# Statistics of x1 moved from the front of the scan's tile to its middle, and the last four normalisations shared between VectorE and ScalarE

## The reference, cut to what matters

```python
x = layernorm(x + attn(x))       # attn: h = x + mamba2(rmsnorm(x)); h + relu(rmsnorm(h) @ w_fc)**2 @ w_proj
x = layernorm(x + ffn(x))        # ffn: silu(x@w1)*(x@w2), two 1024x1024 gelu layers, @ w3
layernorm: (x - mean) / sqrt(var + 1e-5), over the 256 columns of a row
```

## Time and profile before

| what | us |
|---|---|
| median of 3 runs (1225.24 to 1225.66) | 1225.28 |
| the profiled execution, its own time | 1226.21 |
| its span, first to last instruction | 1224.5 |
| scan: one tile of the hardware loop | 66.6 |
| scan and its head, up to the FFN phase | about 568 |
| TensorE busy over the span | 1195.6 |
| VectorE busy over the span | 783.8 |
| GpSimd busy over the span | 237.7 |
| granted clock of TensorE, mean | 0.996 |

### The profile page before, as it was taken

One profiled execution on the slowest core, in us unless ns is written; L12 is line 12 of the kernel. 1 busy time (PEld: TensorE's weight loads), 2 busy tenths in 40 slices (PEclk: granted clock), 3 DMA queues, 4 the chain that ended last, 5 costly groups with the idle time before them and its releaser, 6 DMA issues.

```text
span 1224.5 us, 19168 instructions
## 1 busy us (share of the span) xinstructions
PE 1195.6 (98%) x6412; PEld 1003.1 (82%) x6412; DVE 783.8 (64%) x1370; ACT 639.2 (52%) x1199; POOL 237.7 (19%) x210
## 2 busy tenths in 40 slices
PE   8899999999999999999999999999999999999996
PEld 7677888888887888788888888888888888888885
DVE  6798898989999898855535337345363363543633
ACT  6687888878788878666224124142141331422420
POOL 0517253443435261720000000000000000000000
PEclk9999999999999999999999999999999999999998
DMA  8214131333324141334500202002002020020000
GB/s 294 71 65 126 65 81 72 105 99 101 105 78 128 58 124 64 99 128 172 211 1 1 52 1 51 0 0 51 0 6 45 0 51 0 0 51 0 18 1 19
DMA packets 92169, 79.40 MB, mean 65 GB/s; under 512 B 63200, under 2 KB 81760, under 8 KB 90208
## 3 DMA queue, kind: packets, MB, share of 16 engines
q1 hardware_dynamic: 92128, 78.86, 20.8%
HBM read 66.77 MB, written 25.70 MB: 76 GB/s over the span
## 4 chain that ended last, share of the span: by engine, by line
issue 53%; POOL 0%; DVE 0%; POOLq 0%; DVEq 0%
POOL rsv_b L1937 0%; DVE o_sb L2014 0%; POOLq L1935 0%; DVEq L1768 0%; POOL rsv L237 0%; POOLq L450 0%
## 5 line engine op out<-in xcount | busy, mean ns | idle before, releaser
L1921 ACT ACTIVATE full<-bank,scale 128x512 f32<-128x512 f32 x128 | 88.3, 690 | 383.0 <-PE bank L1830 383.0
L1830 PE MATMUL bank<-hB_hi,h_sb 128*128 128x512 f32 x512 | 199.6, 390 | 0.0
L1830 PE MATMUL bank<-hB_lo,h_sb 128*128 128x512 f32 x512 | 199.6, 390 | 0.0
L1830 PE MATMUL bank<-hA_hi,h_sb 128*128 128x512 f32 x512 | 199.3, 389 | 0.0
L1830 PE MATMUL bank<-hA_lo,h_sb 128*128 128x512 f32 x512 | 199.3, 389 | 0.0
L1983 DVE CAST hA_hi<-full 128x512 fp32r<-128x512 f32 x64 | 27.3, 427 | 173.1 <-ACT full L1921 173.1
L1937 POOL TENSOR_TENSOR rsv_b<-mv_b,eps 128x4 f32<-128x4 f32 x8 | 10.7, 1340 | 618.2 <-DVE mv_b L189 618.2
L1830 PEld LDWEIGHTS bank<-hA_hi,h_sb 128*128 128x128 f32 x512 | 96.1, 188 | 20.1
L1830 PEld LDWEIGHTS bank<-hA_lo,h_sb 128*128 128x128 f32 x512 | 96.1, 188 | 20.1
L1830 PEld LDWEIGHTS bank<-hB_hi,h_sb 128*128 128x128 f32 x512 | 96.3, 188 | 19.2
L1830 PEld LDWEIGHTS bank<-hB_lo,h_sb 128*128 128x128 f32 x512 | 96.2, 188 | 19.0
(11 more groups left out here) (231 smaller groups left out, 2967.6 us busy)
## 6 DMA issues: line engine op xcount, KB each, us to landing
chk_xh<-w_ffn SPq DMA_DIRECT2D x16, 704.0 KB, 4.2
ffn_raw<-w_ffn SPq DMA_DIRECT2D x8, 1408.0 KB, 7.0
h_sb<-ffn_raw SPq DMA_DIRECT2D x2, 4096.0 KB, 19.0
xT<-x_t SPq DMA_DIRECT2D x8, 512.0 KB, 3.9
x_res<-x SPq DMA_DIRECT2D x8, 512.0 KB, 3.8
x_rows<-x SPq DMA_DIRECT2D x8, 512.0 KB, 3.5
x_in<-x_rows SPq DMA_DIRECT2D x8, 512.0 KB, 4.7
x_in<-x SPq DMA_DIRECT2D x7, 512.0 KB, 4.7
```

What stands on the lines that cost most here:

```text
L1830: ins = pe.matmul(o, a_, b_, start=first and n == 0, stop=last and n == 1, skip_group_check=True)
L1921: nc.scalar.activation(full[:, n % FULL, :], b[:], ACT.Gelu, scale=scale[:, 1 + n // KH, n % KH:n % KH + 1]).then_inc(s_gd, 1)
```

## The change

Scan: `norm_x1` leaves the front of DVE's iteration. Its four `bn_stats` (`stats_x1`) and its seven small instructions (`norm_x1_tail`) go, one right behind the other, between `add_out 1` and `yT 2`. On POOL `x1_rstd` goes from between `decay 1` and `u 2` to between `m_lo 6` and `ud 3`. This holds for tiles 2 to 7. `norm_x1` stays as it is for tile 6 (after the scan) and tile 7 (in the FFN phase).

Last FFN tile: the mean's sign is turned (the sum is multiplied by -0.5), so that DVE adds it; DVE scales chunks 0, 1 and 2; POOL computes one more small product, mean times reciprocal deviation (`shift_b`), and ACT scales chunk 3 as `Identity(x * rsv + shift)`. SPq's second store waits for DVE's third chunk and for ACT's.

```diff
@@ POOL, iteration
                     decay_state(i, 1)
-                    if norm:
-                        x1_rstd(pool, i - 2)
                     make_u(w, i, 2)
...
                     if mlp:
                         m_lo_part(i - 1, 6)
+                    if norm:
+                        x1_rstd(pool, i - 2)
                     if more:
                         make_ud(w, i, 3)
@@ DVE, iteration
-                    if norm:
-                        norm_x1(dve, i - 2)
                     mask_exponents(w, 0)
...
                     add_out(w, i, 1)
+                    if norm:
+                        x1_step = stats_x1(dve, i - 2)
+                    if norm:
+                        norm_x1_tail(x1_step)
                     yT(w, 2)
@@ new on DVE
+        def stats_x1(dve, t):
+            step = Steps(dve, s_ls, STAT_STEPS * t)
+            dve.wait_ge(s_pjd, CH * t + CH + 1)
+            for c in range(CH):
+                step.mark(nc.vector.bn_stats(bn[:, c, :], x1[:, c, :]))
+            return step
+        def norm_x1_tail(step):
+            step.wait(step.n)
+            layer_norm_tail(step, bn, mv, EPS_LN).then_inc(s_mv, 1)
@@ SP, last tile
-                    sp.wait_ge(s_o, CH * i + 2 * n + 2)
+                    sp.wait_ge(s_o, CH * i + 2 + n)
+                    if n == 1:
+                        sp.wait_ge(s_oact, 1)
@@ ACT, end
+                act.wait_ge(s_rsb, TILES + 1)
+                c = CH - 1
+                nc.scalar.activation(o_sb[:, c, :], o_sb[:, c, :], ACT.Identity, scale=rsv_b[:, c:c + 1],
+                                     bias=shift_b[:, c:c + 1]).then_inc(s_oact, 1)
@@ POOL, end
+                pool.wait_ge(s_rsb, TILES)
+                nc.gpsimd.tensor_tensor(shift_b[:], mv_b[:, 0, :], rsv_b[:], ALU.mult).then_inc(s_rsb, 1)
@@ DVE, finish_last
-                    layer_norm_tail(step, bn_b, mv_b, EPS_LN).then_inc(s_mvb, 1)
+                    layer_norm_tail(step, bn_b, mv_b, EPS_LN, -0.5).then_inc(s_mvb, 1)
                     dve.wait_ge(s_rsb, i + 1)
-                    for c in range(CH):
+                    for c in range(CH - 1):
                         nc.vector.tensor_scalar(o_sb[:, c, :], o_sb[:, c, :], mv_b[:, 0, c:c + 1], rsv_b[:, c:c + 1],
-                                                ALU.subtract, ALU.mult).then_inc(s_o, 1)
+                                                ALU.add, ALU.mult).then_inc(s_o, 1)
```

More of the change, by code:

```diff
@@ L179, in layer_norm_stats, with layer_norm_tail @@
             return layer_norm_tail(step, bn, mv, eps)
-        def layer_norm_tail(step, bn, mv, eps):
+        def layer_norm_tail(step, bn, mv, eps, half=0.5):
             tt, ts = nc.vector.tensor_tensor, nc.vector.tensor_scalar
@@ L185, in layer_norm_tail @@
             step.link(tt(mv[:, 1, :], bn[:, :, 2], bn[:, :, 5], ALU.add))
-            step.mark(ts(mv[:, 0, :], mv[:, 0, :], 0.5, None, ALU.mult))
+            step.mark(ts(mv[:, 0, :], mv[:, 0, :], half, None, ALU.mult))
             step.mark(tt(mv[:, 2, :], mv[:, 2, :], mv[:, 2, :], ALU.mult))
@@ L227, in sum_x1 @@
                     scalar=r2h[:, c:c + 1], in1=xh[:, c, :], op0=ALU.mult, op1=ALU.add).then_inc(s_pjd, 1)
+        def stats_x1(dve, t):
[7 more added lines that the diff above has]
+            layer_norm_tail(step, bn, mv, EPS_LN).then_inc(s_mv, 1)
+            assert step.n == STAT_STEPS
         def norm_x1(dve, t):
@@ L1744, in post_ln_block @@
         bn_b, mv_b = sb("bn_b", [P, CH, 6]), sb("mv_b", [P, 3, CH])
-        rsv_b = sb("rsv_b", [P, CH])
+        rsv_b, shift_b = sb("rsv_b", [P, CH]), sb("shift_b", [P, CH])
         g_bank = lambda i: banks[i % B_ACT_BANKS]
@@ L1765, in post_ln_block @@
         s_o = sem("out_ready")
+        s_oact = sem("last_rows_out_ready")
         s_store = sem("out_stored")
```

## The result

The changed kernel takes 1234.28 us (median of 4, 1232.21 to 1235.66) against 1225.26 (4 runs, 1224.04 to 1225.66): ratio 1.0073, 95% interval 1.0058 to 1.0088. It is slower, as forecast (1232.6, range 1225.0 to 1236.0). The profiled execution took 1233.96, its span is 1232.3 us against 1224.5.

A forecast was written before the change was run, and what follows sets the result against it. TensorE, busy 98% of the span, bounds the kernel, so only its gaps, set by DVE and POOL holding each other up, can move. 5 x (0.62 + 0.88) - 0.2 = +7.3 on 1225.28 gives 1232.6 us, range 1225.0 to 1236.0.

The forecast's parts named there:

- Part 1, gain at `ydiag 0`: Front of the loop tile: 3.12 us leaving DVE only becomes waiting for POOL's `decay 0`; gain 0, at most 0.23.
- Part 1, `u 2` ahead of `scores 1`: Front: without `x1_rstd`, `u 2` runs first; `scores 1` +0.85, `norm_x` -0.23, so PE loses 0.62 us a tile.
- Part 2: Middle of the loop tile: late POOL instructions hold up DVE's add L1479 and a tap; +0.88 us a tile at `fc0`.
- The work itself is hidden: Middle: the 2.26 us added to DVE fit before `y_diag 3`; `yT 2` ends at 338.8, ahead of 339.06.
- Part 3: End of the kernel: three DVE scalings instead of four end 0.32 us sooner; -0.2 us in the sum.
- B: Rival, chance 0.14: only the middle costs; L1479 gets in ahead of `ud 1` and pays for `scores 1`; 1229.5 us.
- E: Rival, chance 0.11: faster, 1219.5 us; at the front L1479 gets ahead of `ud 1` and `scores 1` ahead of `u 2`.
- C: Rival, chance 0.14: only the front costs; in the middle POOL's two instructions fall between DVE's; 1228.2 us.
- F: Rival, chance 0.08: in the middle one more POOL instruction comes ahead of DVE, 1.88 us a tile; 1237.6 us.

The follow-up runs named there:

- the stand-in: The changed kernel plus an unused POOL power on four columns ahead of `u 2`, where `x1_rstd` had stood: 1228.62 us, ratio 1.0020.
- the last experiment: The kernel before the change with two POOL waits: `ud 1` behind the second add of `y_diag 0`, `u 3` behind `xn_lo`; 1223.7 us, ratio 0.9986.
- 8: The changed kernel with the seven small statistics instructions behind gate 3 on DVE and `x1_rstd` behind `decay 3` on POOL: 1231.6 us, ratio 1.0058.
- 9: The changed kernel with the small statistics instructions behind gate 3, `x1_rstd` behind `decay 3`, and an unused POOL power ahead of `u 2`: 1227.91 us, ratio 1.0023.

## Why the prediction was right

**Part 1, gain at `ydiag 0`: 0.** Right. `scores 0` hangs on POOL's `decay 0`.

**Part 1, `u 2` ahead of `scores 1`: +0.85 - 0.23 = +0.62.** Right in mechanism and size: +0.85 and -0.25 by the rows, 0.61 at PE, 0.58 back with the stand-in, 0.62 with the power alone moved. Only the place was off: PE's loss shows in front of `ydiag 1`, while the gap at L678 shrinks to 0.34 and the one at L592 stays 0.88; the prediction had both grow. It left out that PE itself waits for `scores 1`.

**Part 2, +0.88.** Right mechanism, mis-sized. The two collisions came as forecast (0.27 for 0.3, 0.78 for 0.85; the gate 1.02 late for 1.15), but the slack from the gate to `fc0` is 0.40 and not 0.18 + 0.08. Measured: +0.61. The prediction also let PE lose it all at `fc0`; part of it comes earlier, at the transposes of h (gap of 0.56). "The work itself is hidden" held as well, since it filled idle time; the runs add that the same small instructions put behind that idle time aren't hidden (0.37 and 0.42 a tile), and that taking the collision away gives back 0.24 only.

**Part 3, -0.2.** Wrong in sign in the profile (+0.26), and nothing that a time can tell. ACT's instruction was fast enough; the term that the sum missed is the second wait in front of the store, 0.34 us of issue. ACT started 0.04 us after POOL's product had ended, and its timeline shows no table load in the 8.85 us ahead of it. The Trainium skill (ScalarE: Activation LUTs, Table sets: the hidden batching unit) has identity in every set, and the trace agrees.

**The sum.** 5 x (0.62 + 0.88) = 7.5 was forecast for the loop; 5 x 1.23 = 6.15 measured, by the tiles at full clock. That the time came out 1.7 above the forecast in spite of it has other sources: in the profiled execution some 1.3 of the stretch at lower clock (69.37 - 68.08), and 0.67 of tile 7, the way into the FFN and the end. So the mechanism was right, and that the time lies within 2 us of the forecast is in part luck: a loop put 1.35 too high takes off nearly half of some 3 us that no term of the sum had.

Against the scan part alone (6.5 us) the whole change (9.0) has 2.5 us more, and the end alone shows nothing; the intervals of the two ratios overlap, and the executions of the changed kernel were granted mean clocks of 0.992 to 0.997 where the kernel before had 0.994 to 0.998 beside the last experiment. Stretches at lower clock differ from execution to execution and are worth as much. In the windows of 10 us up to 50 us six of the fourteen traces have them, the kernel before (0.83) and the one after (0.79, 0.86) among them; the scan part alone has 0.52 from 40 to 50, and its first `sum_x1` comes at 162.03, where the eight traces without such a stretch have it between 155.6 and 157.4. But which executions of the changed kernel had one isn't on record, so where these 2.5 us come from stays open. Later than that, only three traces have a stretch, of 0.83 over 10 us: this one, tail behind gate 3 (the tile of 68.92) and power behind `decay 3` (the first tile, 69.48). In the ten microseconds ahead of it PE works at full clock with short gaps in all three (at most 0.7 us idle in any 2 us), and so it does in the scan part alone, where no drop follows; what brings it on wasn't found.

**Rivals.** The toss between L1479 and `ud 1`, on which B and E rest, is real and within 0.02 us. It didn't fall DVE's way here, but did in two tiles with only the power moved. `scores 1` takes 2.06 in those two as well, so they are B's front, in which the one pays for the other (66.52 against 66.63), and not E's, which also wanted `scores 1` ahead of `u 2`. C's condition (front costs, middle free) is the two long tiles of that same kernel. F's power of 1.45 us in the middle didn't come: it took 1.01.

## What to carry to other kernels

An instruction that is taken off a queue was also a spacer: ask what moves up in its place, and whom that meets. On two engines that shut each other out, order is worth as much as work: find pairs that start within a few hundredths of a microsecond and fix the order with a wait in favour of the one that TensorE hangs on. Measure the slack of the path before pricing a delay. Put moved work into an idle time of its engine; right behind that idle time it makes everything later.

## What the runs showed of the hardware

- **A tie within 0.02 us falls either way, and the loser waits nearly as long as the winner works**: the add goes from 0.69 to 1.58 beside a `ud 1` of 1.04, `xn_lo` from 1.22 to 2.10 beside a `u 3` of 1.05. One program has both outcomes in neighbouring tiles. The recorded starts don't tell the winner: `u 3` lost at 314.82 against 314.83, and won at 247.94 against 247.96. The Trainium skill (SBUF — State Buffer, Who interferes with whom) has the exclusion, and the trace agrees; that such a toss can set the time of a whole tile is what the runs add.
- **POOL's power on four columns didn't shut out DVE's instructions with two SBUF inputs**, though it runs 1.0 to 1.5 us: `scores 1` starts beside it and takes 1.21, and three taps beside it take 2.08 in 8 and 9, where they take 2.07 without. It is itself the longer one there, 1.45 or 1.49 instead of 1.01.
- **A VectorE TENSOR_SCALAR with one SBUF tensor is blocked too**, on 4 columns: L186, 0.90 us instead of 0.17. The same section of the Trainium skill counts `tensor_scalar` among those that can take the shared ports; the trace agrees.
- **A second semaphore wait ahead of a store cost 0.34 us of issue** on SP's queue (1.26 against 0.92 for the pair).
- **A gap between weight loads isn't the matmuls' loss**: gaps of 1.02 us ahead of the transposes of h and `fc0` stand for 0.61 of the tile.
- POOL's product on four columns takes 0.20 us, where the power takes 1.01.
